# Attention and feed-forward layer: three stretches of TensorE work cut into 64-row steps behind two units each, and the output projection a turn later

## The reference, cut to what matters

```
xn  = layernorm(x)
q, k, v = xn @ wq + bq, xn @ wk + bk, xn @ wv + bv        # 16 heads of 8
att = softmax(q k^T / sqrt(8)) v                          # per batch and head, 256 x 256
a   = concat_heads(att) @ wo.T + bo
xp  = xn moved by one token;  xr = mu_r*xn + (1-mu_r)*xp;  xk = mu_k*xn + (1-mu_k)*xp
f   = sigmoid(xr @ W_r.T) * (relu(xk @ W_k.T)^2 @ W_v.T)
y   = x + a + f
```

## Time and profile before

| | us |
|---|---|
| median of 3 runs | 483.36 (479.1 to 484.01) |
| the profiled execution | 477.82 |
| its span, first to last instruction | 476.0 |

### The profile page before, as it was taken

The page is one execution under the profiler, slowest core; times in us unless marked ns, Lnnn a source line. Parts: engine busy times, 40 slices in busy tenths (PEclk is TensorE's granted clock), DMA queues, the critical chain, the costliest instruction groups (busy, mean ns, idle before and its releaser), DMA issues. The chain is left out here.

```text
span 476.0 us, 15644 instructions
## 1 busy us (share of the span) xinstructions
PE 444.1 (93%) x5238; PEld 272.0 (57%) x5238; DVE 402.4 (85%) x823; ACT 393.3 (83%) x866; POOL 367.9 (77%) x675
## 2 busy tenths in 40 slices
PE   5698999999999999999999999999999999999994
PEld 4244656565656656565666566566655565666541
DVE  7488898888989998899999888899998889988920
ACT  2047988989888898989888889898898898988883
POOL 6577888888878898788888888788897888876321
PEclk8579999999999999999999999999999999999998
DMA  4444355454344544453455454344554443445100
GB/s 142 134 125 125 104 147 157 127 147 141 111 122 145 156 141 138 121 145 113 127 154 149 139 148 124 102 142 135 156 154 124 149 127 111 129 135 147 47 15 22
DMA packets 85836, 60.42 MB, mean 127 GB/s; under 512 B 6192, under 2 KB 73392, under 8 KB 85808
## 3 DMA queue, kind: packets, MB, share of 16 engines
q1 hardware_dynamic: 85808, 60.06, 44.1%
HBM read 29.89 MB, written 29.36 MB: 124 GB/s over the span
## 5 line engine op out<-in xcount | busy, mean ns | idle before, releaser
L524 DVE TENSOR_REDUCE neg_max<-bank_max 128x2 f32<-128x512 f32 x512 | 328.2, 684 | 44.6 <-PE bank_max L645 40.1
L425 ACT ACTIVATE probs<-bank_exp 128x512 f32<-128x512 f32 x512 | 278.7, 600 | 25.4 <-PE bank_exp L635 24.1
L635 PE MATMUL bank_exp<-ops 51*128 51x256 bf16 x1024 | 156.9, 272 | 4.1 <-issue 3.0
L645 PE MATMUL bank_max<-ops 48*128 48x256 bf16 x1024 | 159.2, 276 | 0.0
L584 PE MATMUL bank_val<-probs,val 128*25 128x256 f32 x2048 | 138.1, 383 | 1.2 <-ACT probs L425 1.2
L635 PEld LDWEIGHTS bank_exp<-ops 51*128 51x128 bf16 x1024 | 75.0, 94 | 77.0 <-issue 65.2
L584 PEld LDWEIGHTS bank_val<-probs,val 128*25 128x25 f32 x2048 | 55.8, 103 | 41.6 <-issue 20.2
L645 PEld LDWEIGHTS bank_max<-ops 48*128 48x128 bf16 x1024 | 76.4, 95 | 5.2
L335 POOL TENSOR_SCALAR xn<-x_in,moments,rstd 128x128 f32<-128x128 f32 x62 | 49.4, 804 | 0.0
L374 POOL TENSOR_TENSOR mixed_x<-mixed_x,xn_t 128x512 f32<-128x512 f32 x32 | 40.7, 1272 | 2.5
L386 POOL TENSOR_TENSOR y<-projected,rest 128x256 f32<-128x256 f32 x32 | 23.4, 732 | 21.7 <-ACT projected L458 21.7
(11 more groups left out here) (67 smaller groups left out, 635.1 us busy)
## 6 DMA issues: line engine op xcount, KB each, us to landing
ops<-spill SPq DMA_DIRECT2D x128, 192.0 KB, 3.4
spill<-qk_h SPq DMA_DIRECT2D x64, 192.0 KB, 3.3
spill<-qk_m SPq DMA_DIRECT2D x64, 128.0 KB, 2.0
x_in<-x SPq DMA_DIRECT2D x32, 128.0 KB, 2.2
spill<-qk_l SPq DMA_DIRECT2D x32, 128.0 KB, 1.8
y_out<-y SPq DMA_DIRECT2D x32, 128.0 KB, 1.9
ops<-shift SPq DMA_DIRECT2D x128, 6.0 KB
w<-weights SPq DMA_DIRECT2D x1, 448.0 KB, 3.2
```

What stands on the lines that cost most here:

```text
L425: nc.scalar.activation(probs[g % 2][:, u % G, :, :], bank_exp[u % 2][:, :, :], ACT.Exp, scale=SCALE).then_inc(exp_done[u], 1)
L524: nc.vector.tensor_reduce(out=neg_max[hf][:, :, r, pr], in_=bank_max[MAX_BANK[v]][:, :, :], axis=AX_X, op=ALU.max, negate=True).then_inc(m ...
L635: exp_mm = nc.tensor.matmul(bank_exp[r][:, i, :], ops[p][rows, hf, 1, pr, i * P:(i + 1) * P], ops[p][rows, hf, 0, pr, :], start=True, stop ...
L645: max_mm = nc.tensor.matmul(bank_max[MAX_BANK[v]][:, i, :], of[rows, max_hf, 0, max_pr, i * P:(i + 1) * P], of[rows, max_hf, 1, max_pr, :] ...
```

## The change

On TensorE:

- The stretches at u=3 (gate and tokens), u=7 (ffn and the transposes of xn and att) and u=15 (projections) become pairs of half stretches, behind units 6 and 7, 10 and 11, 14 and 15. In each half, one piece of work uses the lower 64 rows and one bank, another the upper 64 rows and the other bank; in the second half they swap. A float32 matmul is accumulated from its two halves of rows; a transpose of 64 rows gives 64 columns of the output.
- The second chunk of gate (i=1) and of ffn (i=1) stays whole (128 rows) and goes behind mix 0 (u=5) and mix 1 (u=9).
- The output projection of a batch runs one turn later, at u=3, with values and hidden, which come from u=11.
- In the stretch of u=1 mix 3 goes first and the transposes of the shift second. At u=9 the transposes go first.
- There are new waits of TensorE for its own matmuls (`gate_half`, `tokens_half`, `ffn_half`, `xn_t_half`, `qk_half`). Those for `tokens_half` and `xn_t_half` stand ahead of units 7 and 11, the others ahead of the second half of their work.

On the others: VectorE takes both `qk_rest` behind the reduction of u=0, the statistics at u=3 and 5, att at u=7, ffn at u=12. ScalarE copies projected, val and act_r behind u=3, gate behind u=7, the shift behind u=8, xn_t and att_t behind u=11. GpSimd does `act_sq` behind `qk_l`, then the split of the first maxima, `rest` and `y` of batch `t-2`. SyncE stores batch `t-2`. There is one more turn at the end.

```diff
-T_FIRST, T_LAST = -4, B
+T_FIRST, T_LAST = -4, B + 1
... (PE)
-                nc.tensor.matmul(far[:, 0:S], w[:, W_K, :], moving, start=True, stop=True).then_inc(qk_psum[1], 1)
-                nc.tensor.matmul(near[:, 0:S], w[:, W_Q, :], moving, start=True, stop=True).then_inc(qk_psum[0], 1)
+                nc.tensor.matmul(far[:, 0:S], w[LOWER, W_K, :], moving[LOWER, 1:1 + S], start=True,
+                                 stop=False).then_inc(qk_half[1], 1)
+                nc.tensor.matmul(near[:, 0:S], w[UPPER, W_Q, :], moving[UPPER, 1:1 + S], start=True,
+                                 stop=False).then_inc(qk_half[0], 1)
+            def project_end(c, n):
+                pe.wait_ge(qk_half[1], n(3))
+                nc.tensor.matmul(far[:, 0:S], w[UPPER, W_K, :], moving[UPPER, 1:1 + S], start=False,
+                                 stop=True).then_inc(qk_psum[1], 1)
+                pe.wait_ge(qk_half[0], n(3))
+                nc.tensor.matmul(near[:, 0:S], w[LOWER, W_Q, :], moving[LOWER, 1:1 + S], start=False,
+                                 stop=True).then_inc(qk_psum[0], 1)
+            def gate_rows(rows, i, p, bank, start, stop):
+                return nc.tensor.matmul(bank[:, i * D:(i + 1) * D], mixed_x[p][rows, 0, i * P:(i + 1) * P],
+                                        w[rows, W_R, :], start=start, stop=stop)
+            def tokens_rows(rows, bank):
+                for st in range(ST):
+                    for i in range(2):
+                        k = (ST * st + i) * P
+                        last = nc.tensor.transpose(bank[:, k + rows.start:k + rows.stop],
+                                                   mixed[rows, i, st * P:(st + 1) * P], ident[rows, rows])
+                return last
...
+                    if u == 7 and live(-1):
+                        pe.wait_ge(tokens_half, n(-1))
+                    if u == 11 and live(3):
+                        pe.wait_ge(xn_t_half, n(3))
...
+                    if u == 5 and live(0):
+                        mix_values(0, n(0), n(-1), p)
+                        after(pe, val_done, n(1))
+                        pe.wait_ge(act_r_done, n(0))
+                        gate_rows(BOTH, 1, p, near, True, True)
...
+                    if u == 6 and live(0):
+                        gate_rows(LOWER, 0, p, near, True, False).then_inc(gate_half, 1)
+                    if u == 6 and live(-1):
+                        tokens_rows(UPPER, far).then_inc(tokens_half, 1)
+                    if u == 7 and live(-1):
+                        tokens_rows(LOWER, far).then_inc(tokens_psum, 1)
+                    if u == 7 and live(0):
+                        pe.wait_ge(gate_half, n(0))
+                        gate_rows(UPPER, 0, p, near, False, True).then_inc(gate_psum, 1)
+                    if u == 9 and live(1):
+                        pe.wait_ge(max_split[0], n(1))
+                        after(pe, gate_done, n(0))
...
+                        transpose_shift(0, near)
+                    if u == 9 and live(0):
+                        mix_values(1, n(0), n(-1), p)
...
+                        ffn_rows(BOTH, 1, near, True, True)
...
+                    if u == 10 and live(0):
+                        ffn_rows(LOWER, 0, near, True, False).then_inc(ffn_half, 1)
+                    if u == 10 and live(-1):
+                        last = att_t_rows(UPPER, far)
+                    if u == 10 and live(3):
+                        xn_t_rows(UPPER, far).then_inc(xn_t_half, 1)
+                    if u == 11 and live(-1):
+                        att_t_rows(LOWER, far).then_inc(att_t_psum, 1)
+                    if u == 11 and live(3):
+                        xn_t_rows(LOWER, far).then_inc(xn_t_psum, 1)
+                    if u == 11 and live(0):
+                        pe.wait_ge(ffn_half, n(0))
+                        ffn_rows(UPPER, 0, near, False, True).then_inc(ffn_psum, 1)
+                    if u == 14 and live(3) and (live(1) or not live(2)):
+                        project_begin(c, n, live)
                     if u == 15 and live(3) and (live(1) or not live(2)):
-                        project(c, n, live)
+                        project_end(c, n)
```

More of the change, by code:

```diff
@@ L323, in step @@
                 if live(3) and live(2):
[L324 to L333, removed]
                     for i in range(ST):
@@ L381, in step @@
                     nc.gpsimd.tensor_tensor(rstd[:, :], var_eps[:, :], minus_half[:, :], ALU.pow).then_inc(rstd_done, 1)
[L382 to L387, removed]
+                if live(4):
+                    pool.wait_ge(rstd_done, n(4))
+                    after(pool, xn_t_psum, n(3))
                 if live(1):
@@ L537, in step @@
                                                 ALU.mult).then_inc(att_done, 1)
[L538 to L544, removed]
+                    if u == 11 and live(3) and not live(2):
+                        dve.wait_ge(weights_in, 16 * N_WEIGHT_DMAS)
+                        dve.wait_ge(ident_made, 1)
+                        fill_constants()
+                    if u == 12 and live(0):
                         dve.wait_ge(ffn_psum, n(0))
                         dve.wait_ge(gate_done, n(0))
-                        after(dve, xn_t_done, n(3))
                         after(dve, rest_done, n(-1))
@@ new lines, in xn_t_rows, with att_t_rows @@
+            def xn_t_rows(rows, bank):
+                for i in range(ST):
+                    last = nc.tensor.transpose(bank[:, i * P + rows.start:i * P + rows.stop], xn[rows, i, :],
+                                               ident[rows, rows])
+                return last
+            def att_t_rows(rows, bank):
+                for st in range(ST):
+                    k = S + st * P
+                    last = nc.tensor.transpose(bank[:, k + rows.start:k + rows.stop],
+                                               att[rows, st * H:(st + 1) * H].rearrange("p k e -> p (k e)"),
+                                               ident[rows, rows])
+                return last
@@ L656, in step @@
                         transpose_shift(1, near)
[L657 to L660, removed]
+                    if u == 3 and live(-2):
+                        pe.wait_ge(att_t_done, n(-2))
+                        after(pe, qk_rest_done[0], n(2))
+                        if not live(2):
+                            after(pe, ffn_done, n(-1))
+                        for i in range(ST):
+                            last = nc.tensor.matmul(far[:, i * D:(i + 1) * D], att_t[:, i * P:(i + 1) * P],
+                                                    w[:, W_O, :], start=True, stop=True)
+                        last.then_inc(wo_psum, 1)
@@ L666, in step @@
[L666 to L671, removed]
-                                k = ST * st + i
-                                last = nc.tensor.transpose(far[:, k * P:(k + 1) * P],
-                                                           mixed[:, i, st * P:(st + 1) * P], ident[:, :])
-                        last.then_inc(tokens_psum, 1)
@@ L676, in step @@
-                    if u == 5 and live(0):
-                        mix_values(0, n(0), n(-1), p)
-                    if u == 7 and live(0):
-                        pe.wait_ge(act_sq_done, n(0))
-                        pe.wait_ge(gate_done, n(0))
-                        for i in range(ST):
-                            last = nc.tensor.matmul(near[:, i * D:(i + 1) * D], act_sq[:, i * P:(i + 1) * P],
-                                                    w[:, W_VV, :], start=True, stop=True)
-                        last.then_inc(ffn_psum, 1)
@@ L685, in step @@
-                    if u == 7 and live(3):
-                        pe.wait_ge(xn_done, n(3))
-                        after(pe, qk_rest_done[1], n(2))
-                        for i in range(ST):
-                            last = nc.tensor.transpose(near[:, S + i * P:S + (i + 1) * P], xn[:, i, :], ident[:, :])
-                        last.then_inc(xn_t_psum, 1)
-                    if u == 7 and live(-1):
-                        pe.wait_ge(att_done, n(-1))
-                        for st in range(ST):
-                            last = nc.tensor.transpose(far[:, st * P:(st + 1) * P],
-                                                       att[:, st * H:(st + 1) * H].rearrange("p k e -> p (k e)"),
-                                                       ident[:, :])
-                        last.then_inc(att_t_psum, 1)
```

193 lines of the change are left out of this document (112 added, 81 removed).

## The result

The changed kernel takes **501.69 us** (500.23 to 502.19, 4 runs) against 481.6 for the kernel before (479.1 to 484.01, 4 runs): ratio 1.041, 95% interval 1.034 to 1.048. The forecast was slower, 495.6 us in a range of 471 to 507. I had 12.2 us of loss; it is 20 against the median of 481.6 (18.3 against the 483.36 that I started from).

What follows compares the result with a forecast made beforehand. TensorE was taken as the bound. The turn: 12.75 + 0.60 + 0.10 + 0.34 + 0.20 = 13.99 us, 0.37 more; 31 turns give 11.5, plus 0.7, 12.2 us in all: 495.6 us, range 471 to 507.

Steps and rivals of the forecast that it cites:

- waits ahead of units 7 and 11: TensorE waits for the last half transpose, so each unit starts at 0.60 and not 0.43 us: 0.34 a turn.
- waits for `probs` at units 9 and 13: These units, and unit 1, each wait 0.20 us for an exponential: 0.60 a turn.
- paid neighbourhoods: Whole chunks of gate and ffn behind column strips at u=5 and u=9 pay extra: 0.10 us each, bounds nothing to 0.19.
- Half transposes: In the halves of gate/tokens and ffn/xn/att, four half transposes load 128 columns each: 4 x 0.11 = 0.43 us, gap 0.54.
- Rival 1: Faster: 64-row transposes cost 0.055, halves 6 and 10 shorten, neighbourhoods free; turn 13.03, 466 us. Chance 0.22.
- my own last sign: The forecast is wrong if units never wait for `probs`, or if half transposes stand 0.055 us apart.
- The wait's price: Before a unit waiting on a half transpose, 0.05 us passes from the awaited work's end to the waiter's start.
- The chain of 1.08: Unit u+2 needs u's exponential: 0.43 us until it starts, 0.60 for it, then 0.05, together 1.08.
- The 0.10 at unit 3: At a turn's start ScalarE's queue frees unit 3 at 2.57 us, TensorE wants it near 2.49: 0.1 late.
- Projections: Crosswise halves behind units 14 and 15 make gaps of 0.11 + 0.43 = 0.54 us each, without load or way in and out.
- the 0.7 that I gave it: The extra turn's output work and two more completions in the last chain cost 0.7 us in all.
- the prediction's bare sum: A turn's gaps, halves and units without new waits or neighbourhoods: 12.75 us, 0.87 less than before.

Runs made afterwards that it cites:

- run 1: The changed kernel with the waits for the half transposes behind units 7 and 11, second gate or ffn half issued first: 484.44 us, ratio 1.018.
- Run 2: The changed kernel without the whole chunks of gate and ffn (i=1) behind mix 0 and mix 1, their outputs left out: 474.71 us, ratio 0.991.
- run 3: The kernel before with only the projections of q and k in crosswise halves behind units 14 and 15: 494.29 us, ratio 1.033.
- run 5: The changed kernel with the transposes of the shift ahead of mix 3 again at u=1: 526.95 us, ratio 1.095.
- run 8: The changed kernel with gate, tokens, ffn, xn, att and projections whole again; order of u=1, later output projection and moved copies stay: 476.6 us, ratio 0.991.
- run 7: The kernel before with each gate matmul cut into two of 64 moving columns: 487.52 and 493.2 us in two executions, ratio 1.022.
- run 6: The kernel before with one edit, mix 3 ahead of the transposes of the shift at u=1: 475.85 us, ratio 0.990.
- run 9: As run 8, but VectorE takes k's `qk_rest` at u=15 again and only q at u=0: 470.47 us, ratio 0.982.
- run 10: As run 9, but gate, tokens, ffn, xn and att in halves, with the waits for halves behind units 7 and 11: 482.26 us, ratio 1.006.

## Why the prediction was right, point by point

The sign and the three mechanisms that I named were right: waits ahead of units 7 and 11, waits for `probs` at units 9 and 13, paid neighbourhoods. The turn was to be 13.99 and is 14.14. By gaps, forecast and measured, the wait of the next unit included:

| gap | forecast | after |
|---|---|---|
| u=1 | 1.29 | 1.44 |
| u=3 (unit 3 late) | 1.72 + 0.10 | 1.72 |
| u=5 | 1.51 | 1.61 |
| 6 to 7, 10 to 11 | 0.71 | 0.66 |
| 7 to 8, 11 to 12 | 0.54 | 0.37 |
| 8 to 9, 12 to 13 | 0.31 | 0.47 |
| u=9 | 1.61 | 1.70 |
| 14 to 15 | 0.54 | 0.55 |
| 15 to 0 | 0.54 | 0.68 |
| 0 to 1 | 0.31 | 0.16 |

- **Half transposes** were mis-sized: 0.06 apart and not 0.11. I gave them a matmul's load. The row that shows better, 328 against 272 ns, was in the kernel before. It moved no total: behind units 6 and 10 the wait was dearer instead, 0.30 and not 0.17 (run 1: 0.36 without it, 0.66 with it), and behind units 7 and 11 the shorter halves came back as longer waits of units 9 and 13, 0.84 for gap and wait together against 0.85 forecast. That the two totals agree so well is in part luck: two errors went against each other. Rival 1 was right on its premise and wrong on what follows. So was my own last sign: half transposes 0.055 apart were to show the forecast wrong, and they stand 0.06 apart, but the dearer waits took back what they save. For the same reason unit 7 stands 0.55 behind the half's first matmul (282.99 to 283.54), not 0.6 to 0.7.
- **The wait's price**: 0.05 from end to start was read at ScalarE's exponential, and only to the load of the waiting unit. Here the end of the last half transpose (283.40) and unit 7 (283.54) are 0.14 apart.
- **Neighbourhoods**: 0.20 each, not 0.10, the upper bound. From the last of mix 0's four rounds of 0.22 to the chunk are 0.31, and the first load is naked (377 ns against 275). Run 2 has the sum. The Trainium skill ("TensorEngine Tiling (Array Packing)", Key Properties) says that a change of tiling mode drains the engine; the trace agrees with it, with 0.09 on this way.
- **The chain of 1.08** held: units 7 to 9 are 1.06 apart. The 0.10 at unit 3 did not appear.
- **Projections**: the first half came as forecast (0.55); the second costs 0.13 more than that, its loads stand behind a wait and are naked (`L625` lasts 0.47 and then 0.38). What I priced at nothing, k ready only with the second half, turned out the largest effect of that edit in run 3; in the changed kernel mix 3 hides it (run 5), all but 0.15.
- **The sum** was short by 10.2 us in the span (12.2 forecast, 22.4 measured). The turn has 4.3 of it (31 times 0.51 and not 0.37). The other turns have 1.4. The loop's end costs 0.54 in the changed kernel, five times; in the kernel before it is 0.15 at the last three, 0.3 at the second and 1.0 at the first, so the five cost 1.0 less there. The last three turns differ by 1.05 more than three regular ones do, and the first turns by 0.6 less. With halved projections the loop's end took 0.5 in all six such kernels, with whole ones 0 (run 8), 0.15 (run 7) or 0.3 (runs 6, 9 and 10) in the later passes. The short last piece of work ahead of the branch may have a part in it; no run shows that by itself, and the size is not settled. The end took 0.8 more than the 0.7 that I gave it.
- **The start** has the other 3.7 us; I had nothing there. It goes with the clock. From 30 to 40 us TensorE has a granted clock of 1.00 in the kernel before and of 0.50, the lower of its two levels, in the changed one, and does 107 matmul instructions against 56. From 20 to 30 us, just ahead of the rise in the kernel before, it was busy for 8.6 us there and for 8.3 us in the changed kernel. Whether the change has any part in this is not shown. Runs 8 and 9, alike but for VectorE's order, differ in the same way: the first copy of `mixed` stands at 51.3 and 47.0, and the unit matmuls between 30 and 39 us last 409 and 306 ns on average, against 272 in the kernel before and 412 in the changed one. The clock column of run 8 says 1.00 there, so it is the durations that have to be read.

## What to carry to other kernels
Splitting work to save a way in and a way out pays only if nothing in the neighbourhood takes its place: add up the naked loads, the chunks that can't be split, and the waits for one's own completions. A wait belongs behind independent work, not ahead of it: its place was worth 0.54 us a turn here. That is as much as all the splitting could give by the prediction's bare sum (0.87 less the 0.37 of the order at u=1). And look first at what waits: exchanging two blocks that stood in the wrong order gave 1%, and together with the later output projection and the moved copies, k still taken early, 1.8%.

## What the runs showed of the hardware that was not expected
- A float32 transpose's weights load in about half the time of a float32 matmul's (0.056 against 0.10 us naked, both 128 columns and 128 rows); half transposes of 64 rows follow each other in 0.06 us, and matmuls of 64 moving columns no faster than 0.11 us.
- A matmul of 64 rows that stands behind a wait has the same naked load as one of 128 rows: 373 against 272 ns, and 377 against 275. Halving the rows did not shorten it. The Trainium skill ("TensorE: Matmul & The Clock Gate", LDWEIGHTS) says that loads go by columns, not by the contraction rows, and here the trace agrees. By that rule a transpose's load of 128 columns would cost what a matmul's does; it costs 0.056 and not 0.10, and there the measurement decides.
- From work in column strips to whole-array work TensorE loses 0.09 us (282.03 to 282.34, with rounds of 0.22), as it does from a unit to whole-array work (267.81 to 268.01 in the earlier trace rows, with 0.11 between the unit's matmuls) and from a unit to the strips (281.15 to 281.35).
